# A fused network of a selective scan and attention layers: Silu groups, gates and the next chunk's input projection in other steps of the scan

## What is computed

```python
ada = silu(c) @ ada_w.T + ada_b ;  shift, scale, gate = split(ada, 3)
xn = layernorm(x) * (1 + scale) + shift
x_in, z = split(xn @ in_proj_w.T, 2)
u = silu(causal_conv4(x_in) + conv_b)
dt_r, B, C = split(u @ x_proj_w.T, [64, 80])
dt = softplus(dt_r @ dt_proj_w.T + dt_proj_b) ;  A = -exp(A_log)
# for every time t:
h = h * exp(dt_t * A) + (dt_t * u_t) * B_t
y_t = sum_n(h * C_t)
y = (y + u * D_param) * silu(z)
out = x + gate * (y @ out_proj_w.T)
```

## Time and profile before

| what | us |
|---|---|
| median of 3 runs (lowest, highest) | 6101.4 (6100.11, 6107.05) |
| profiled execution, its own time | 6100.49 |
| span of that execution | 6098.8 |
| TensorE busy in the span | 5423.8 |
| VectorE busy | 4129.5 |
| ScalarE busy | 2840.5 |
| GpSimd busy | 3014.9 |

### The profile page before, as it was taken

One profiled execution on the slowest core, in us unless ns is written; L12 is line 12 of the kernel. 1 busy time (PEld: TensorE's weight loads), 2 busy tenths in 40 slices (PEclk: granted clock), 3 DMA queues, 4 the chain that ended last, 5 costly groups with the idle time before them and its releaser, 6 DMA issues. The chain is left out here.

```text
span 6098.8 us, 61913 instructions
## 1 busy us (share of the span) xinstructions
PE 5423.8 (89%) x20064; PEld 2545.6 (42%) x20064; DVE 4129.5 (68%) x5409; ACT 2840.5 (47%) x4898; POOL 3014.9 (49%) x2032
## 2 busy tenths in 40 slices
PE   6888888888887878989999999999988888889797
PEld 2333333333333334434444444444434354544545
DVE  3999999999999942257777777777735444444353
ACT  4657565565756523315566555655651121212121
POOL 4878787887868731116666666666660000000000
PEclk8999999999999989979999999999999999989899
DMA  4021211202121033221011011111112201020101
GB/s 159 21 97 35 104 70 49 86 33 97 60 79 72 25 122 110 100 59 33 22 33 33 22 32 30 25 33 24 31 43 103 76 14 61 15 98 24 66 24 48
DMA packets 116700, 345.79 MB, mean 57 GB/s; under 512 B 12272, under 2 KB 13520, under 8 KB 102032
## 3 DMA queue, kind: packets, MB, share of 16 engines
q1 hardware_dynamic: 96432, 286.07, 14.3%
q0 software_dynamic: 9216, 33.56, 1.4%
q10 hardware_dynamic: 10784, 22.89, 1.0%
HBM read 274.29 MB, written 67.67 MB: 56 GB/s over the span
## 5 line engine op out<-in xcount | busy, mean ns | idle before, releaser
L1335 DVE TENSOR_REDUCE attn_mx<-attn_ps_max 128x1 f32<-128x512 f32 x2048 | 1270.6, 684 | 439.6 <-PE attn_ps_max L1207 435.1
L1190 POOL TENSOR_TENSOR attn_pair_sum<-attn_prob 128x1024 f32<-128x1024 f32 x512 | 1208.0, 2379 | 671.6 <-ACT attn_prob L1301 671.6
L415 POOL TENSOR_TENSOR mamba_hc<-mamba_h,mamba_bc 128x1024 f32<-128x1024 f32 x512 | 1217.8, 2379 | 414.6 <-DVE mamba_h L627 360.5
L1301 ACT ACTIVATE attn_prob<-attn_ps_s 128x512 f32<-128x512 f32 x2048 | 1060.9, 603 | 624.0 <-PE attn_ps_s L1232 620.4
L766 PE MATMUL mamba_y<-mamba_hc,ident 128*128 128x512 f32 x2048 | 1029.2, 627 | 291.0 <-POOL mamba_hc L415 289.8
L521 ACT ACTIVATE mamba_da<-mamba_dt,mamba_a_neg 128x512 f32<-128x512 f32 x1024 | 690.3, 689 | 763.7 <-DVE mamba_h L627 754.7
L627 DVE TENSOR_TENSOR_SCAN mamba_h<-mamba_da,mamba_state,mamba_h 128x512 f32<-128x512 f32 x768 | 940.9, 1268 | 30.2 <-ACT mamba_da L521 30.2
L1232 PE MATMUL attn_ps_s<-attn_q_stack,attn_k_stack 100*128 100x512 f32 x2048 | 862.2, 424 | 11.6 <-DMA attn_q_stack<-attn_m_parts 5.7
L1207 PE MATMUL attn_ps_max<-attn_k_stack,attn_q_stack 98*128 98x512 f32 x2048 | 836.1, 415 | 16.8 <-DMA attn_q_stack<-qk_parts 16.2
L766 PEld LDWEIGHTS mamba_y<-mamba_hc,ident 128*128 128x128 f32 x2048 | 378.1, 195 | 876.8 <-issue 458.0
L617 DVE TENSOR_TENSOR mamba_h<-mamba_du,mamba_bc 128x1024 f32<-128x1024 f32 x512 | 619.9, 1211 | 69.5 <-POOL mamba_state L417 63.0
(11 more groups left out here) (223 smaller groups left out, 6039.5 us busy)
## 6 DMA issues: line engine op xcount, KB each, us to landing
mamba_bc<-bc_dram SPq DMA_DIRECT2D x64, 1024.0 KB, 9.1
mamba_w<-in_in_proj_w_T SPq DMA_DIRECT2D x16, 2048.0 KB, 8.0
qk_parts<-qkv_pair POOLq DMA_DIRECT2D x64, 512.0 KB
attn_k_stack<-qk_parts SPq DMA_DIRECT2D x96, 256.0 KB
attn_q_stack<-qk_parts SPq DMA_DIRECT2D x96, 256.0 KB
mamba_x_in<-in_x SPq DMA_DIRECT2D x16, 1024.0 KB, 5.5
mamba_w<-in_out_proj_w_T SPq DMA_DIRECT2D x8, 2048.0 KB, 9.2
lin_norm_x<-x_after_L SPq DMA_DIRECT2D x16, 1024.0 KB, 5.6
```

The costliest lines, as they stand in the source:

```text
L415: nc.gpsimd.tensor_tensor(hc[:, gs % HC_SLOTS, :, :], h[:, gs % H_SLOTS, :, :], bc[:, g, G:2 * G, :], ALU.mult).then_inc(s["hc_done"], 1)
L1190: nc.gpsimd.tensor_tensor(pair_sum[p % 2][:, at], prob[2 * p % SLOTS][:, at], prob[(2 * p + 1) % SLOTS][:, at], ALU.add).then_inc(s["sum_d ...
L1301: nc.scalar.activation(prob[kt % SLOTS][:, c * CH:(c + 1) * CH], ps_s[n % BANKS][:, :], ACT.Exp).then_inc(s["exp_done"], 1)
L1335: nc.vector.tensor_reduce(mx[hd % 3][:, qt, kc:kc + 1], ps_max[seq % BANKS][:, :], AX.X, ALU.max).then_inc(s["bank_read"], 1)
```

## The change

```diff
--- before.py
+++ after.py
@@ -190,17 +190,17 @@
         BACK_LATE = {3: (0, 3), 4: (1, 3)} | {5 + n: (2 + n // 4, n % 4) for n in range(8)}
         Z_AT = {13 + n: divmod(n, 2) for n in range(2 * CT)}
         TR = 29
-        IN_AT = {32 + n + n // 3: divmod(n, 2) for n in range(2 * CT)}
-        XP_AT = {54 + n: n for n in range(4)}
-        DT0 = 59
+        IN_AT = {31 + n + n // 3: divmod(n, 2) for n in range(2 * CT)}
+        XP_AT = {53 + n: n for n in range(4)}
+        DT0, SPLIT = 58, 59
         DT_AT, READ, SOFT_AT, ADD_AT = 2, 2, 5, 4
         STATS, RSTD, NORM = 23, 24, 27
         OUT_READ = [7, 8, 12, 16]
         Z_COPY = [14 + 2 * e + 3 for e in range(CT)]
-        Z_SILU = {22: (0, 1, 2), 29: (3, 4, 5), 33: (6, 7)}
+        Z_SILU = {24: (0, 1, 2), 30: (3, 4, 5), 34: (6, 7)}
         TAP = [i + 3 for i, (e, half) in IN_AT.items() if half]
-        U_SILU = {TAP[2] + 5: (0, 1, 2), TAP[5] + 4: (3, 4, 5), TAP[7] + 3: (6, 7)}
-        GATE = {24: 0, 25: 1, 28: 2, 35: 3, 43: 4, 51: 5, 59: 6}
+        U_SILU = {TAP[3] + 1: (0, 1, 2), TAP[5] + 2: (3, 4), TAP[7] + 3: (5, 6, 7)}
+        GATE = {25: 0, 27: 1, 31: 2, 35: 3, 43: 4, 51: 5, 59: 6}
         CG_AT = {3 + n: divmod(n, KC // 2) for n in range(NB * KC // 2)}
         CG_READ = 13
         GATE_LAST = 2
@@ -572,7 +572,7 @@
                             for e in U_SILU[i]:
                                 silu_u(it + 1, e)
                             back_to_exp()
-                        if i == 60:
+                        if i == SPLIT:
                             split_x(it + 1)
                         if i == DT0 + 3:
                             softplus(it + 1, 0)
```

## The result

| what | before | changed |
|---|---|---|
| median, us | 6100.75 (6098.0 to 6107.05, 4 runs) | 6040.82 (6038.8 to 6046.71, 4 runs) |
| span of the profiled execution | 6098.8 | 6037.2 |
| a middle chunk (scan 0 to scan 0, mean of the six in the middle) | 264.1 | 256.1 |

The ratio is 0.9905, 95% interval [0.9894, 0.9916]: 60 us less, where 55 were forecast. Seven chunks are 8.0 us shorter and the last 3.0: 59 of the span's 61.6. What is left lies outside the chunks, where nothing changed.

The account below looks back on a forecast made before the run. VectorE was taken to set the pace, its waits for ScalarE's decays (41.3 us) and GpSimd's state copies (63.0) being the prize. 23.2 + 5.6 + 8.4 + 17.4 = 54.6 off the median 6101.4 gave 6047 us, range 6036 to 6071.

Parts of the forecast that it names:

- Step 30: ScalarE's three-tile Silu group moves here from step 29; VectorE's 3.08 us wait nearly goes, about 0.1 stays: gain 23.2 us.
- The drain of 1.38 us: Rival at ScalarE's table switches: each drains besides its load, leaving some 2.8 us at step 31: 6069 us, chance 0.02.
- Step 34: ScalarE's two-Silu group moves here, leaving the turns alone in step 33; VectorE's 0.80 us wait goes: gain 5.6 us.
- Window: Steps 34 to 57, GpSimd's taps one step earlier: idle 1.66 and 0.60 filled, less 0.88 and 0.2: gain 8.4 us.
- the 1.63 at scan 54: VectorE's wait for ScalarE there; removing it is worth at most 0.6 us, the rest becoming a wait for GpSimd.
- ScalarE in steps 43 to 46: ScalarE's busiest place: 12.8 us of tap, group, softplus, tap was claimed to fit in four steps of some 4.2 each.
- The taps in time: At step 34 the first tap is ready at 764.1, GpSimd asks at 764.15: margin nothing to 0.2 us.
- The chunk's end: GpSimd's softplus addition moves to step 60, so du starts before the product; 0.34 + 2.15 fall away: gain 17.4 us.
- Sum: Whole kernel: the four gains, 23.2 + 5.6 + 8.4 + 17.4, make 54.6 us.
- Rival 5: Slower: a late first tap at step 34 holds GpSimd, product 35 and VectorE, us for us; 6120 us, chance 0.03.
- The signs named at the end: Over the stage: VectorE's decay waits under 10 us, line 610 never near 2.8, state copies still 45 to 63 us.

Follow-up runs that it names:

- x1: The kernel before with only the groups of silu(z) moved to steps 24, 30, 34 and the gates to 25, 27, 31: 6067.8 us.
- x11: The changed kernel with only the last group of silu(z) back in step 33, ahead of the two turns: 6073.1 us.
- x2: The kernel before with only the group of silu(u) in step 53 moved to 54: 6096.1 us.
- x3: The changed kernel with only GpSimd's addition of softplus 0 moved back from behind product 60 to behind product 61: 6060.1 us.
- x4: The changed kernel with GpSimd's addition of softplus 0 back behind product 61, and GpSimd waiting for du before product 62: 6046.7 us.
- x8: The changed kernel with GpSimd adding only the first three columns of each tile's third tap, from the second chunk on: 6011.7 us.
- x7: The changed kernel with the third tap of all tiles but 3 and 6 on VectorE, one step behind ScalarE's TAP: 6025.7 us.

## Why the prediction held, and where it did not

- *Step 30, 2.9 x 8.* Right, with its working: the decay of step 31 came 0.1 late. The drain of 1.38 us that the Trainium skill, "ScalarE: Activation LUTs", has behind a switch does not show: the group measures 4.28 in both kernels, and x1 has its gain.
- *Step 34, 0.8 x 7.* Right in size (no wait is left). Wrong in what it is worth: x11, which puts only this group back, costs 4.2 a chunk, not 0.8. The term was read as ScalarE against VectorE; that the turns behind the group feed TensorE, and the taps, was not costed.
- *Window, 1.2 x 7.* Measured 98.57 - 97.22 = 1.35. x2 shows the claim that the 1.63 at scan 54 is worth at most 0.6. The du of step 54 did take 1.83. The size is in part luck: GpSimd's idle time fell by 1.03 (98.57 - 94.76 against 97.22 - 94.44), and its busy time, which the prediction took to be the same, by 0.32.
- *ScalarE in steps 43 to 46.* They were reckoned to hold 12.8 us of its work. Not quite: the only wait for decays that the changed kernel has is here, 0.4 at scan 45. It lies within the window, whose 1.35 is already less by it.
- *The taps in time.* "Nothing to 0.2 us" of margin: they were up to 0.2 late, without harm.
- *The chunk's end, 2.5 x 7.* Right, 0.34 + 2.15; x3 and x4 show both parts.
- *Sum.* From scan start to scan start, a middle chunk lost 3.04 at scans 30 and 31, 0.88 at 34, 1.35 in the window, 0.19 between scans 57 and 58, where GpSimd no longer lags, and 2.57 at the end: 8.03, all of it. A wait costs the step some 0.09 more than its length in these rows: with 3.08 ahead of scan 30 the step is 747.29 - 740.64 = 6.65, which is 3.17 over the 3.48.
- *Rival 5.* I gave it 0.03 since ScalarE would have to be "over two steps behind". The mechanism exists, 3.2 us at the first tap, and one table entry brings it (x11), with the turns only 3.8 us late, one group: the projection waits for them, and the tap for it. Its price, a us of the chunk for each us at the tap, held: 3.2 at the tap made 2.63 at scan 36 and 0.64 behind it. To be slower in the whole the tap would have had to be 7.5 late; x11, at 3.2, is still 25 us faster than the kernel before. What kept it away is the part of the change that I had valued at 5.6 us.
- *The parts as a sum.* z alone -31, input projection with the u groups alone +12, both with the dt chain -60. The terms add up only in the order in which the edits make room for one another.
- The signs named at the end held: 2.7 us for decays, line 610 at most 1.84, 56.8 for the state copies.

## What to carry to other kernels

Cost a moved piece along its whole chain, not only against the engine that sets the pace: the same group one step later was worth 0.8 us by the wait in front of it, and 4.2 with the projection behind it. Where a bounded buffer ties two engines, spread the work of the feeding engine evenly over the steps; its sum tells what can be had at best, and x8, which only made the sum smaller, got half of it. Two engines that exclude each other are cheap when the one that sets the pace is let go first, which a wait in the right place can arrange.

## What the runs showed of the hardware

The exclusion is long enough to plan for: du took 0.68, 1.23 (x8), 1.70, 1.84 or 2.83 us, by where it met GpSimd. Where the two started within 0.02 us of each other it went either way: in seven chunks of the changed kernel the du of step 38 took 1.84 and that of step 46 took 0.68, there with GpSimd's tap stretched to 1.8 instead. A scalar_tensor_tensor of VectorE with one operand in PSUM took 0.71 to 0.72 us in x7, all 42 times while GpSimd was at work. And TensorE's clock fell at the end of its wait of 3.87 us in x11. Four pieces of the projection took 3.65 us there, and 1.88 five us later (the rows of x11 above). The view of stretches, of TensorE's wait and of the time behind it (the number ahead of the DMA share is the granted clock as a share of 2.4 GHz):

```profile
748.35:754.20 5.85, 1.98 (x4) 0.70 (x5) 5.58 (x5) 5.79 (x8) 5.05 (x5) 1.00 0.89 325
754.20:760.00 5.80, 5.79 (x10) 2.56 (x11) 5.28 (x5) 2.40 (x4) 3.65 (x4) 0.71 0.01 4
```

0.71 is a mean over a stretch that began at 1.2 GHz and ended at 2.4. In the stretch that holds the wait the clock was granted in full, so TensorE lost its wait and, behind it, 1.8 us more. This is no price of the late turns alone, though. In the same chunk of the changed kernel TensorE waits 2.04 us for GpSimd's product of step 35, which stands behind the first pair of taps, and then runs slowly, too:

```profile
753.07 3.40 PE L766 MATMUL mamba_y<-mamba_hc,ident 128*128 128x512 f32 x4 [2.04 <-POOL mamba_hc L415]
```

```profile
752.60:756.10 3.50, 3.03 (x4) 1.45 (x5) 3.22 (x4) 3.35 (x6) 3.50 (x5) 0.52 0.00 0
```

Over the whole program both profiled executions have a mean granted clock of 0.961.
